# A table of steps: three batches first, the last batch's search spread over steps, relu parts spread over the Gram stage

## The reference

```python
sq = jnp.sum(xyz * xyz, axis=1)
d2 = sq[:, :, None] + sq[:, None, :] - 2.0 * jnp.einsum('bdn,bdm->bnm', xyz, xyz)
_, idx = jax.lax.top_k(-d2, k)                      # k = 8
...
for i in range(NUM_BLOCKS):                         # 4, run twice
    shortcut = points
    p = _lrelu(points)                              # slope 0.01
    g = _group_point(p, idx_t)
    c = jnp.einsum('oi,bin->bon', w_center[i], p)
    gn = jnp.einsum('oi,bikn->bokn', w_neighbor[i], g)
    points = (c + gn.sum(axis=2)) / (K + 1.0) + shortcut
```

## Time and profile before

| | us |
|---|---|
| median of 3 runs | 359.35 (356.36 to 360.37) |
| the profiled execution | 357.09 |
| its span, first to last instruction | 355.3 |
| TensorE busy in the span | 337.2 |
| VectorE / ScalarE / GpSimd busy | 227.6 / 116.2 / 79.3 |
| mean granted clock of TensorE, 1 is 2.4 GHz | 0.986 |

### The profile page before, as it was taken

How to read it: one execution, slowest core, us unless ns; L and a number is a source line. 1 busy time by engine, 2 the same in 40 slices (tenths; PEclk the granted TensorE clock), 3 DMA queues, 4 the chain that set the end, 5 groups by cost and what they waited for, 6 DMA issues and landing times.

```text
span 355.3 us, 4392 instructions
## 1 busy us (share of the span) xinstructions
PE 337.2 (95%) x1816; PEld 270.5 (76%) x1816; DVE 227.6 (64%) x314; ACT 116.2 (33%) x133; POOL 79.3 (22%) x43
## 2 busy tenths in 40 slices
PE   5999938999999998699999999999999999999997
PEld 2667616666666678588898898898898898988985
DVE  0146149437835856886876777776777767767764
ACT  1114451202111121136445345354354354353320
POOL 2002520000000000022432523423423424324300
PEclk9999996999999999989999999999999999999999
DMA  7994430343321000000000000000000000000033
GB/s 255 329 341 169 148 118 0 120 148 118 120 79 68 1 2 0 2 1 0 2 0 2 0 2 0 0 2 0 3 0 2 0 0 2 0 2 0 2 118 118
DMA packets 7442, 20.19 MB, mean 57 GB/s; under 512 B 640, under 2 KB 1920, under 8 KB 6400
## 3 DMA queue, kind: packets, MB, share of 16 engines
q1 hardware_dynamic: 7424, 19.93, 16.4%
HBM read 17.83 MB, written 2.10 MB: 56 GB/s over the span
## 4 chain that ended last, share of the span: by engine, by line
PE 87%; ACT 4%; DVE 4%; POOL 2%; DVEq 1%; DMA 1%; issue 1%; ACTq 0%
PE wide L313 33%; PE wide L229 26%; PE wide L292 8%; PE wide L294 8%; PE wide L302 8%; POOL r_low L212 2%; ACT relu L413 1%; PE wide L236 1%; PE wide L280 1%; ACT r_high L418 1%; DMA points<-in_ctx_dram 1%; DVE y_rest L540 1%; DVEq L526 1%; ACT w_low L436 1%; PE wide L265 1%
## 5 line engine op out<-in xcount | busy, mean ns | idle before, releaser
L212 POOL TENSOR_TENSOR r_low<-relu,r_high 128x1024 fp32r<-128x1024 f32 x32 | 77.0, 2407 | 255.9 <-ACT r_high L418 255.9
L229 PE MATMUL wide<-points 128*128 128x512 f32 (+3 forms) x384 | 111.9, 446 | 3.6 <-DMA points<-in_ctx_dram 3.6
L313 PE MATMUL wide<-adj,y_hi 128*128 128x512 f32 (+1 forms) x260 | 102.6, 396 | 3.2 <-DVE state L551 3.2
L313 PE MATMUL wide<-adj,y_lo 128*128 128x512 f32 (+1 forms) x260 | 102.4, 395 | 0.0
L229 PEld LDWEIGHTS wide<-points 128*128 128x128 f32 x384 | 66.6, 195 | 39.2 <-issue 21.0
L413 ACT ACTIVATE relu<-state 128x1024 f32<-128x1024 f32 x32 | 33.9, 1061 | 112.4 <-DVE state L551 104.6
L292 PE MATMUL wide<-w_high,r_high 128*128 128x256 f32 x256 | 62.5, 283 | 1.7 <-DVE y_rest L540 1.0
L294 PE MATMUL wide<-w_low,r_low 128*128 128x256 f32 x256 | 62.4, 282 | 0.0
L540 DVE TENSOR_TENSOR y_rest<-wide,y_hi 128x1024 f32<-128x1024 f32 x32 | 39.2, 1225 | 33.0 <-ACT y_hi L423 33.0
L313 PEld LDWEIGHTS wide<-adj,y_hi 128*128 128x128 f32 x260 | 49.5, 190 | 13.6 <-DVE state L551 3.4
L313 PEld LDWEIGHTS wide<-adj,y_lo 128*128 128x128 f32 x260 | 49.4, 190 | 10.2
(11 more groups left out here) (51 smaller groups left out, 139.2 us busy)
## 6 DMA issues: line engine op xcount, KB each, us to landing
points<-in_ctx_dram SPq DMA_DIRECT2D x8, 1024.0 KB, 5.4
points<-in_ctx_dram SPq DMA_DIRECT2D x8, 256.0 KB, 3.3
points<-in_ctx_dram SPq DMA_DIRECT2D x4, 512.0 KB, 5.1
state<-in_x_dram SPq DMA_DIRECT2D x4, 512.0 KB, 13.5
out_dram<-state SPq DMA_DIRECT2D x3, 512.0 KB, 2.8
rest<-in_ctx_dram SPq DMA_DIRECT2D x8, 128.0 KB, 5.2
w_raw<-in_fside_BxSxS_dram SPq DMA_DIRECT2D x1, 1024.0 KB, 12.5
last_row<-in_ctx_dram SPq DMA_DIRECT2D x1, 1024.0 KB, 17.0
```

The source lines that it names most:

```text
L212: nc.gpsimd.tensor_tensor(r_low[:, b, :, :], relu[:, :, :], r_high[:, b, :, :].bitcast(fp32), ALU.subtract).then_inc(r_low_ready, 1)
L229: mm = nc.tensor.matmul(bank[i][:, 0:N - i * P], points[:, t, i * P:(i + 1) * P], points[:, t, i * P:N], start=(t == 0), stop=False)
L313: mm = nc.tensor.matmul(bank[to][:, cols], part[:, b % 2, q, h * P:(h + 1) * P], adj[:, b, q, cols], start=(q == 0 and part is y_hi), stop ...
```

## The change

The order of the steps becomes a table, `STEPS`, made by a small rule. Steps 0 to 6 go round batches 0, 1, 2 only. From step 7 on batch 3 joins, and the rule takes the batch with the most layers left that isn't one of the last two. The table begins (0,0) (0,1) (0,2) (1,0) (1,1) (1,2) (2,0) (0,3) (2,1) (2,2) (1,3), each a layer and a batch; a batch comes again after 3, 4 or 5 steps, where it was always 4. The search of batch 3 is spread: its distances behind step 0's `split_y`, one `neighbours` call in each of the iterations 2 to 5, `turn_neighbours` behind step 7. At the start only batch 0's relu parts are made; those of batches 1 and 2 follow the first two batches' `copy_adj`. `weights_mixed` moves behind the first batch's search. The waits and places of the step loops are written anew:

```diff
--- before.py
+++ after.py
+        ENTER = 7
+        STEPS = []
+        for s in range(B * LAYERS):
+            recent = [b for _, b in STEPS[-2:]]
+            left = {b: LAYERS - sum(1 for _, c in STEPS if c == b) for b in range(B if s >= ENTER else B - 1)}
+            b = s % (B - 1) if s < ENTER else max((b for b in left if b not in recent), key=lambda b: (left[b], b == B - 1, -b))
+            STEPS.append((LAYERS - left[b], b))
+        def out_at(s):
+            return EVEN_WIDE if s < ENTER or s % 2 == 0 else ODD_WIDE
...
             def y_step(s, w, b, first=False):
 
-                pe.wait_ge(r_mixed_ready, s + 1)
+                pe.wait_ge(r_low_ready, s + 1)
                 if not first:
                     pe.wait_ge(y_rest_ready, s)
...
                 mm.then_inc(main_done, 1)
+                pe.wait_ge(r_mixed_ready, s + 1)
                 if not first:
                     pe.wait_ge(y_lo_ready, s)
...
-            for l in range(1, LAYERS):
-                for b in range(B):
-                    y_step(l * B + b, l % BLOCKS, b)
-                    if b == 0:
+            for s, (l, b) in enumerate(STEPS):
+                y_step(s, l % BLOCKS, b, first=(s == 0))
+                if s == 0:
+                    square_row(B - 1)
+                else:
+                    if s - 1 == STEPS.index((0, B - 1)):
                         pe.wait_ge(adj_ready, 2 * B)
+                    if s - 1 == ENTER:
+                        pe.wait_ge(state_ready, s - 1)
+                    elif s - 1 > 0:
+                        pe.wait_ge(state_ready, s - 1 if out_at(s - 1) == out_at(s - 2) else s - 2)
+                    out_step(s - 1, STEPS[s - 1][1], out_pieces(s - 1))
+                if s == 1:
+                    turn_distances(B - 1)
+                if s == ENTER:
+                    turn_neighbours(B - 1)
-            pe.wait_ge(state_ready, LAYERS * B - 2)
-            out_step(LAYERS * B - 1, B - 1, LAST_OUT)
+            pe.wait_ge(state_ready, LAST_STEP)
+            out_step(LAST_STEP, STEPS[LAST_STEP][1], LAST_OUT)
...
-            for b in range(B):
-                make_relu(b, b)
-                relu_high(b, b)
+            relu_parts(0)
...
                 copy_adj(b)
-            for s in range(B, B * LAYERS):
-                n = s + 2
-                if n < B * LAYERS:
-                    make_relu(n, n % B)
-                y_high(s, s % B)
-                if n < B * LAYERS:
-                    relu_high(n, n % B)
+                if b < B - 2:
+                    relu_parts(b + 1)
+            for s in range(B * LAYERS):
+                if s + 1 >= B - 1 and s + 1 <= LAST_STEP:
+                    relu_parts(s + 1)
+                y_high(s)
+                if s == 1:
+                    copy_low(B - 1)
+                if s == ENTER:
+                    copy_adj(B - 1)
...
-            for s in range(B, B * LAYERS):
-                update(s - 2, (s - 2) % B, EVEN_WIDE if s % 2 == 0 else ODD_WIDE)
-                n = s + 1
-                if B < s < B * LAYERS - 1:
-                    relu_mixed(n, n % B)
-                split_y(s, s % B)
-            update(LAYERS * B - 2, B - 2, EVEN_WIDE)
-            update_last(LAYERS * B - 1, B - 1)
+            for s in range(B * LAYERS):
+                split_y(s)
+                if s == 0:
+                    distances(B - 1)
+                if s > 0:
+                    update(s - 1)
+                if B - 1 <= s + 1 <= LAST_STEP:
+                    relu_mixed(s + 1)
+                if 2 <= s < 2 + NB:
+                    neighbours(B - 1, s - 2)
+            update_last(LAST_STEP)
```

More of the change, by code:

```diff
@@ L108, in knn_blocks_kernel, with step_before @@
         ALL = slice(0, N)
[L109 to L112, removed]
         LAST_OUT = ((0, ALL, 4), (1, slice(0, N // 2), 5), (1, slice(N // 2, N), 0))
+        ENTER = 7
[5 more added lines that the diff above has]
+            STEPS.append((LAYERS - left[b], b))
+        LAST_STEP = B * LAYERS - 1
+        FINAL = [STEPS.index((LAYERS - 1, b)) for b in range(B)]
+        assert sorted(STEPS) == [(l, b) for l in range(LAYERS) for b in range(B)]
+        def step_before(s):
+            l, b = STEPS[s]
+            return STEPS.index((l - 1, b))
+        def out_at(s):
+            return EVEN_WIDE if s < ENTER or s % 2 == 0 else ODD_WIDE
         points_in = [sem(f"points_in_{n}") for n in range(len(LOADS))]
@@ L189, in _ @@
                 load_rest(b)
[L190 to L195, removed]
+            for s in sorted(FINAL):
+                b = STEPS[s][1]
+                if s < LAST_STEP:
+                    sp.wait_ge(state_ready, s + 1)
+                    sp.dma_start(out[b, :, :].rearrange("(h p) n -> p h n", p=P), state[:, b, :, :])\
+                      .then_inc(stored, 16)
+                else:
+                    for n, (h, cols, _) in enumerate(LAST_OUT):
+                        sp.wait_ge(state_ready, s + n + 1)
+                        sp.dma_start(out[b, h * P:(h + 1) * P, cols], state[:, b, h, cols]).then_inc(stored, 16)
             sp.wait_ge(stored, 16 * (B - 1 + len(LAST_OUT)))
@@ L213, in relu_low @@
                                         ALU.subtract).then_inc(r_low_ready, 1)
-            for n in range(B * LAYERS):
-                relu_low(n, n % B)
+            for n, (l, b) in enumerate(STEPS):
+                relu_low(n, b)
         @block.tensor
@@ L312, in out_step, with out_pieces @@
                         for part in (y_hi, y_lo):
-                            mm = nc.tensor.matmul(bank[to][:, cols], part[:, b % 2, q, h * P:(h + 1) * P],
+                            mm = nc.tensor.matmul(bank[to][:, cols], part[:, s % 2, q, h * P:(h + 1) * P],
                                                   adj[:, b, q, cols], start=(q == 0 and part is y_hi),
                                                   stop=(q == NB - 1 and part is y_lo))
-                    if n == len(pieces) - 1 or len(pieces) > 2:
+                    if s == LAST_STEP or n == CH - 1:
                         mm.then_inc(out_done, 1)
+            def out_pieces(s):
+                return LAST_OUT if s == LAST_STEP else tuple((h, ALL, 2 * out_at(s) + h) for h in range(CH))
             for i in range(NB):
@@ L572, in _ @@
                 rest_low(b + 1)
+                distances(b)
+                for i in range(NB):
+                    neighbours(b, i)
                 if b == 0:
```

74 lines of the change are left out of this document (18 added, 56 removed).

## The result

The changed kernel takes 393.61 us (median of 4, 391.25 to 397.14) against 358.61 us for the kernel before on the same chip. The forecast was 369.5 us with a range up to 374.5. The direction was right, the size was not: +34.3 us (392.86 - 358.61) where +11.2 was worked out.

The account below looks back on a forecast made before the run. TensorE, busy throughout the steady stretch, was taken as the bound. -9.6 - 4.9 + 22.4 + 1.8 + 1.5 = +11.2 us gave 368.3 from the profiled execution, 370.6 from the median; forecast 369.5, range 364.0 to 374.5 us.

Parts of the forecast that it names:

- Part 1: Start of the kernel: relu parts leave it, so the 7.0 us wait for the first distances goes; -9.6 us.
- Part 2: Batch 3's search is spread: step 1's OUT no longer waits for step 0's update, -4.9 us.
- zero, at most 0.3 us each: Cost of the four spread neighbours calls in iterations 2 to 5, where VectorE would otherwise wait for ScalarE.
- Part 3: relu_mixed stands behind update, both under one MAIN: MIXED waits 0.80 us a step, 28 steps, +22.4 us.
- start plus both operations is 2.56 us whatever else VectorE does: Update and r_mixed behind OUT's end take 2.56 us, against MAIN's 1.90 us.
- does something else hold TensorE longer?: Check of a batch that comes again after 3 steps: all in time, y_lo by 0.5 us.
- a second wait joins: Rival: y_lo late or a smaller front gain, 1 to 6 us more, 371 to 376 us; chance 0.10.
- The clock: Rival: granted clock falls at the new 0.8 us waits; 419 us if at each, 375 if one in ten; chance 0.04.
- Part 4: copy_adj behind step 7 makes step 9's MIXED wait 1.8 us in place of 0.80, +1.0 us.
- Part 5: The last OUT now waits for step 30's update, with nothing to cover it; +1.5 us.

## Why the prediction was wrong

**Part 1, -9.6 us: right.** From the first row of squares to the second 29.26 us; 9.4 and 8.5 us measured alone.

**Part 2, -4.9 us for the first update: right; "zero, at most 0.3 us each" for the spread search: wrong.** In the profile after no wait for the state of step 0 is left and the clock is 1.00 there. Its 4.9 us were not measured by themselves; the sum below closes with them to 0.2 us. What failed for the search is the length of a call, taken as "at most 2.6 us" from a stretch in which GpSimd did nothing. Now the `nbr` in each call met `r_low` and took 2.5 to 2.8 instead of 0.69 us, so the steps 3 to 7 came 8.8, 8.8, 8.8 and 9.5 us apart instead of 7.4: 6.4 us in all. That VectorE would otherwise wait for ScalarE there was right: with short `nbr` these steps are 7.40 us apart.

**Part 3, 0.80 us a step: right for what it priced** (0.81), and this is why the kernel is slower at all: 28 x 0.81 = 22.7 us. The step that failed is "start plus both operations is 2.56 us whatever else VectorE does", and with it the answer to "does something else hold TensorE longer?": both left out what GpSimd does to VectorE. Seven times `r_mixed` met `r_low` and took 3.13 instead of 1.21 us, 13.4 us in all, for which the prediction's sum had nothing. GpSimd's work was placed only for the tightest case, a batch that comes again after 3 steps, where it lies clear. Directly behind it, where the next batch comes again after 5 steps and has more slack, it collided. The rival "a second wait joins" had the kind, but at 1 to 6 us.

**The clock** took 3.0 us of the profiled execution, in two stretches behind waits of 2.5 us: two steps of 10.86 and 10.75 us among the `r_mixed` starts where others of that kind have 9.32. The prediction gave this rival a chance of 0.04. It came true in part, but by another way than it was put: not at the waits of 0.8 us, where the clock stood at 1.00, but only where contention had made the waits long. The rule of the Trainium skill, "TensorE: Matmul & The Clock Gate", section "A second HAM failure mode: psum-queue depth-cycling", is thus borne out here for waits of 2.45 us, and not for those that cost 0.8 us.

**Part 4, +1.0 us: too high.** MIXED of step 9 (timeline of the changed kernel) waits 0.83 us where other steps have 0.55, so 0.3 us more. MIXED of step 8 doesn't wait at all, since turning the neighbours stands ahead of it on TensorE; that is why there are 28 waits and not 29.

```profile
199.10 1.21 PE L322 MATMUL wide<-w_mixed,r_mixed 128*128 128x256 f32 x8 [0.83 <-DVE r_mixed L471]
```

**Part 5, +1.5 us: right**, 1.3, by the wait in the groups above and by the run without it.

**The sum.** The two profiled executions are 391.0 and 355.3 us long, 35.7 apart. The pieces read from their rows are -9.6 (rows of squares), -4.9 as forecast, +22.7 for 28 waits, +1.3 at the end, +13.4 for the seven `r_mixed`, +6.4 for the search and +3.0 of clock, together +32.3. Another 3.2 us lie ahead of the first row of squares (43.92 against 40.71 us). They are not the change's: every version that shares its Gram stage has that row between 40.14 and 43.92 us, and the row differs by 2.9 us between two executions of the version with the Gram stage's change alone. So +35.5 of the 35.7 us are placed. By the medians, +34.3 us is 8.4 for the parts forecast and priced right, 1.3 for part 5, and 24.6 that the two versions with GpSimd held back took away (20.7 and 3.9), where the prediction had nothing.

**Could it have been read?** Yes, from the trace before. One VectorE operation with two inputs in SBUF had met `r_low` in it, at the start, where nobody waited (timeline of the kernel before):

```profile
31.36 0.29 DVE L505 SCALAR_TENSOR_TENSOR half_diag<-gram,ident 128x128 f32<-128x128 f32 x1
...
32.09 2.35 POOL L212 TENSOR_TENSOR r_low<-relu,r_high 128x1024 fp32r<-128x1024 f32 x1 [29.07 <-ACT r_high L418]
...
32.77 1.82 DVE L505 SCALAR_TENSOR_TENSOR half_diag<-gram,ident 128x128 f32<-128x128 f32 x1
```

The same operation takes 0.29 us alone and 1.82 beside `r_low`, ending 0.15 us behind it. The other order stands a few rows further on, where the next `r_low` begins during a VectorE operation with both inputs in SBUF and takes 2.55 us, not 2.35:

```profile
36.42 0.69 DVE L511 TENSOR_TENSOR diag_lo<-half_diag,diag_hi 128x512 fp32r<-128x512 f32 x1
...
36.77 2.55 POOL L212 TENSOR_TENSOR r_low<-relu,r_high 128x1024 fp32r<-128x1024 f32 x1 [2.32 <-ACT r_high L418]
```

The prediction used neither. The median of the first group, 0.29 us, hides it; its longest doesn't. The Trainium skill says in "SBUF — State Buffer", section "Who interferes with whom", that a VectorE instruction with both inputs in SBUF contends with a GpSimd instruction that reads SBUF, not with one that only writes it, and that the order in which the two are issued decides which one is blocked. The runs here agree, with 2.45 us behind the two-input operation, 1.22 beside memsets, and the copy of 2.07 us for the reverse order.

## What to carry to other kernels

When a change moves an operation or lets one start earlier, lay GpSimd's reading operations and VectorE's operations with two SBUF inputs side by side in the new order, for every kind of step and not only the tightest; look in the trace for the longest of each group, not only the mean. An operation that stands directly behind the producer of a long stretch and ahead of its consumer has lost its slack, however short it is: 2.56 us under 1.90 us cost 0.81 us in each of 28 steps and outweighed both gains. If a change has parts, try the part off the steady stretch by itself: here it alone was worth 2.4%.

## What the runs showed of the hardware

- GpSimd's operations that read SBUF and VectorE's with two inputs in SBUF exclude each other by whole instructions, in the order of their starts. Behind a GpSimd operation with two inputs, `r_mixed` took 2.45 or 3.13 instead of 1.22 us. Behind a VectorE operation with two inputs, `r_low` took 3.19 instead of 2.40 and a one-input copy 2.07 instead of 1.03 us. A one-input copy ahead of `r_mixed` was not tried.
- VectorE's operations with one input from PSUM (update 1.23 us) and GpSimd's memsets (0.96 us) are not touched.
- Waits that cost 0.81 us in every step of 7.4 us left the granted clock at 1.00 over 227 us. Waits of about 2.45 us in every step lowered its mean to 0.89 over 300 us, behind 19 of 28 waits.
